# A graph layer's groups taken in a new order, and the last experts' slots cut finer, in one fused kernel

## Chip, cores and metric

One NeuronCore of one Trainium2 chip runs the whole program. The metric is the device time of one execution in microseconds. TensorE (PE) has a granted clock with two levels here, 1.2 and 2.4 GHz, which the profile writes as 0.5 and 1.0.

## The reference

The input is `x`, 128 sequences of 64 tokens with 128 features each (8192 tokens), in float32. Four layers follow, each as `x = x + layer(layernorm(x))`:

1. a spectral graph layer (an eigenbasis of the adjacency, two dense products);
2. a mixture of 8 experts with the top 2 of each token;
3. the second graph layer with an LSTM behind it;
4. a mixture of 8 experts with the top 1 of each token, which share one up projection.

The change touches layers 3 and 4, which are:

```python
# layer 3, first part
h = relu(einsum('ts,bsh->bth', adj, x @ Wg0 + bg0))
h = relu(einsum('ts,bsh->bth', adj, h @ Wg1 + bg1))
for p in 1..4:              # LSTM over windows of p tokens, last state written back
    ...
# layer 4
H = gelu(xf @ W1 + b1)                    # 128 -> 512, one W1 for all experts
probs = softmax(H @ Wg + bg); assign = argmax(probs)
out[token] = probs[token, e] * (H @ Wd[e] + bd[e])   for e = assign[token]
```

## The kernel before

The 8192 tokens are 64 tiles of 128 (`TILES`), and four tiles are a group (`GC` = 512 columns), so there are 16 groups (`GROUPS`). Each layer is a block with a program of its own for each engine; the engines meet at semaphores only, each engine runs its program in the written order, and a block ends before the next begins. `X` (all tokens) stays in SBUF.

**`gnn1` (L1420 to L1605)** is the second graph layer together with the step p = 1 of the LSTM. Its stages for a group g are:

- POOL (L1444) gathers for each token tile two rows of the first experts' result by an indirect DMA (128 gathers in all). There are 8 pairs of buffers (`AHEAD`), so POOL may be two groups ahead.
- DVE `combine` adds both to `X` (L1456, L1458), `stats` takes the tile's statistics (L1463), `scale` (L1469 to L1479, with the inverse root of L1411 to L1417) makes mean and scale of the group.
- ACT `normalized` writes `ZB` (L1529, four instructions). PE makes MIX from it (L1585), ACT copies it to `ZS` (L1553), PE makes UP (L1590, L1591), ACT's ReLU gives HT (L1561), PE makes DN (L1597), DVE `add_bias` gives O (L1487), PE makes MIX2 (L1604), ACT's ReLU gives HS (L1565).
- PE makes the three LSTM gates from HS (GATE, L1576), ACT `gate` applies sigmoid and tanh (L1539), DVE `new_cell` multiplies (L1495), ACT takes the tanh (L1556), DVE `new_state` writes the state into `BIG` (L1500).

The order is written out by hand. PE's turn g is: GATE of group g-1, then MIX, UP, DN and MIX2 of group g. ACT's turn g is: normalized g, gate g-1, ZS g, tanh g-1, HT g, HS g. DVE's turn g is the four tiles of group g; behind the second tile's comes new_cell g-2, behind the third's new_state g-2 and then add_bias g-1; scale g is last.

**`route` (L1101)** gives each token a slot in a list ordered by expert, in which each expert's part is rounded up to whole blocks of `SLOT_TILE` = 256 slots. DVE makes from the counts a table of blocks (`fill`, L1152 and L1154, with `most` = 32 multiples of 256), the slots, and the expert of each block (`te`, L1176 and L1178, with `tiles` x 8 elements on one partition). A loop of one-hot products on DVE, ACT and PE (L1189, L1204, L1218) then lists the tokens by slot, `cols_` columns wide. It is called for layer 2 ("r", 71 tiles of 256) and for layer 4 ("t", 39 tiles of 256, 78 columns).

**`experts` (L1224)** runs over the tiles of 256 slots: POOL gathers the tokens in two halves (L1250, L1254), PE transposes them (L1318), ACT copies (L1292), PE makes the up projection (L1333), ACT's Gelu writes `H` (L1304), PE makes the down projection (L1346) with the weights of the tile's expert, whose number it loads into a register (L1339), DVE adds the expert's bias (L1284, the number loaded at L1279), and SP stores (L1357). On PE the order is: up of tile t, transposes of tile t+1, down of tile t-1. For layer 2 ("c") DVE also copies the expert's up weights for each tile (L1266, L1267); layer 4 ("g") has one up matrix (`w_up_all`). `sweep` writes the first three turns out, puts the middle ones into a hardware loop of two turns, and writes the last ones out.

Of the kernel before, what the change touches and what calls it, by code (L numbers as in the profile page):

```python
# [6 lines left out]
I32 = mybir.dt.int32  # L7
# [4 lines left out]
ds = bass.ds  # L12
# [17 lines left out]
SLOTS0 = (2 * B * N + E * (SLOT_TILE - 1)) // SLOT_TILE * SLOT_TILE  # L30
SLOTS1 = (B * N + E * (SLOT_TILE - 1)) // SLOT_TILE * SLOT_TILE
CONSTS = 11 + E
# [1067 lines left out]

def route(nc, k, sem, tag, choices, slots):  # L1101

# [3 lines left out]
    n = len(choices)  # L1106
    cols_, tiles = slots // P, slots // SLOT_TILE
    most = B * N // SLOT_TILE
    RANK, TOT, LIST, SEATS = k.ps[0], k.ps[1], k.ps[2], k.ps[3]
    s_kept = sem(f"{tag}_kept")  # L1110
    DEEP = 4
    with ExitStack() as own:  # L1112
# [14 lines left out]
        zero = mine("zero", [P, cols_])  # L1127
        block = own.enter_context(nc.Block())

        @block.vector  # L1130
        def _(dve):
# [10 lines left out]
            link(dve.tensor_scalar(steps[:, :], k.irow[:, 0:most], float(SLOT_TILE), None, ALU.mult))  # L1142

# [13 lines left out]
            link(dve.tensor_tensor(off[:, :], end[:, :], nb[:, :], ALU.subtract))  # L1157
            link(dve.scalar_tensor_tensor(out=off[:, :], in0=off[:, :], scalar=float(SLOT_TILE), in1=cnt[:, :],
                                          op0=ALU.mult, op1=ALU.add))
# [36 lines left out]

        @block.scalar
# [9 lines left out]
        @block.tensor  # L1207
        def _(pe):
            pe.wait_ge(marks, 1)
            pe.matmul(RANK[:, :], k.upper[:, :], M[:, :, :].rearrange("p e t -> p (e t)"), start=True, stop=True)  # L1210
            pe.matmul(TOT[:, :], k.ones[:, :], M[:, :, :].rearrange("p e t -> p (e t)"),
                      start=True, stop=True).then_inc(counted, 1)
            pe.matmul(LIST[:, 0:cols_], k.ident[:, :], zero[:, :], start=True, stop=False)
            with pe.Fori(0, TILES * n // DEEP) as i:
                for b in range(DEEP):
                    pe.wait_ge(oh_ready, i * DEEP + (b + 1))
                    pe.wait_ge(ab_ready, i * DEEP + (b + 1))
                    pe.matmul(LIST[:, 0:cols_], above[b][:, :], ohh[b][:, :], start=False, stop=False).then_inc(oh_used, 1)  # L1218
            pe.matmul(LIST[:, 0:cols_], k.ident[:, :], zero[:, :], start=False, stop=True).then_inc(listed, 1)
            pe.wait_ge(s_kept, 1)  # L1220
            pe.matmul(SEATS[:, 0:cols_], k.jump[:, :], summed[:, :], start=True, stop=True).then_inc(listed, 1)


def experts(nc, k, sem, tag, z, y, slots, w_up_all, w_up, w_dn, b_up, b_dn):  # L1224
# [8 lines left out]
    with ExitStack() as own:  # L1233
# [26 lines left out]
        def _(dve):  # L1260
# [9 lines left out]
            def step(t, u, r):  # L1270
# [6 lines left out]
                if not first:  # L1277
                    v, before = 1 - u, r - 1 + u
                    e = dve.value_load(k.expert[0:1, ds(t - 1, 1)], min_val=0, max_val=E - 1)  # L1279
                    dve.wait_ge(dn, t)  # L1280
                    if not (isinstance(before, int) and before < 1):
                        dve.wait_ge(stored[v], before * 16)
                    b2 = b_dn[:, :, :].rearrange("p e d -> p (e d)")[:, ds(e * D, D)]
                    dve.tensor_tensor(ys[v][:, :, :], Y[v][:, 0:HALVES * D].rearrange("p (h d) -> p h d", d=D),  # L1284
                                      b2[:, None, :].to_broadcast([P, HALVES, D]), ALU.add).then_inc(y_ready, 1)
            sweep(dve, step, NT)
# [25 lines left out]
        def _(pe):  # L1312
# [8 lines left out]
            def step(t, u, r):  # L1321
# [16 lines left out]
                if not first:  # L1338
                    e = pe.value_load(k.expert[0:1, ds(t - 1, 1)], min_val=0, max_val=E - 1)  # L1339
                    pe.wait_ge(gelu, t * C)  # L1340
# [3 lines left out]
                    for h in range(HALVES):  # L1344
                        for c in range(C):
                            last = pe.matmul(Y[v][:, h * D:(h + 1) * D], H[v][:, c, h * P:(h + 1) * P],  # L1346
                                             w2[:, ds(e * (C * D) + c * D, D)], start=(c == 0), stop=(c == C - 1))
                    last.then_inc(dn, 1)
# [71 lines left out]
def gnn1(nc, k, sem, y):  # L1420
# [7 lines left out]
    with ExitStack() as own:  # L1428
# [20 lines left out]
        def _(dve):  # L1449
# [52 lines left out]

            for g in range(GROUPS + 2):
                for j in range(GT):
                    if g < GROUPS:
                        combine(g * GT + j)
                        stats(g * GT + j)
                    if j == 1 and g >= 2:
                        new_cell(g - 2)
                    if j == 2:  # L1510
                        if g >= 2:
                            new_state(g - 2)
                        if 1 <= g <= GROUPS:
                            add_bias(g - 1)
                if g < GROUPS:
                    scale(g)
            link.reset()
            dve.wait_ge(hid, GROUPS)

        @block.scalar  # L1520
        def _(act):
# [20 lines left out]

            for g in range(GROUPS + 2):
                u = g % 2
                if g < GROUPS:
                    normalized(g)
                if 1 <= g <= GROUPS:
                    gate(g - 1)
                if g < GROUPS:
# [3 lines left out]
                    act.activation(k.ZS[u][:, :], MIX[u][:, :], ACT.Copy).then_inc(mixed_sb, 1)  # L1553
                if 1 <= g <= GROUPS:
                    act.wait_ge(cell, g)
                    act.activation(tcs[1 - u][:, :], cs[1 - u][:, :], ACT.Tanh).then_inc(tanh_c, 1)  # L1556
                if g < GROUPS:
# [3 lines left out]
                    act.activation(HT[u][:, :], UP[:, :], ACT.Relu).then_inc(h_ready, 1)  # L1561
                    act.wait_ge(mix2, g + 1)
                    if g >= 2:
                        act.wait_ge(fed, g - 1)
                    act.activation(HS[u][:, :], MIX2[:, :], ACT.Relu).then_inc(h2, 1)  # L1565

        @block.tensor
        def _(pe):
            for g in range(GROUPS + 1):
                u = g % 2  # L1570
                if g >= 1:
                    pe.wait_ge(h2, g)
# [4 lines left out]
                    last.then_inc(fed, 1)  # L1577
                if g == GROUPS:
                    break
                pe.wait_ge(z_ready, g + 1)  # L1580
                if g >= 2:
                    pe.wait_ge(mixed_sb, g - 1)
                for j in range(GT):
                    c = slice(j * P, (j + 1) * P)
                    last = pe.matmul(MIX[u][:, c], k.ZB[u][:, c], k.BDAT[:, :], start=True, stop=True)  # L1585
                last.then_inc(mixed, 1)
                pe.wait_ge(mixed_sb, g + 1)
                if g >= 1:
                    pe.wait_ge(h_ready, g)
                pe.matmul(UP[:, :], k.w_g1[:, 0, :], k.ZS[u][:, :], start=True, stop=False)  # L1590
                pe.matmul(UP[:, :], k.b_g1a[:, :], k.adjsum[:, :], start=False, stop=True).then_inc(up, 1)  # L1591
                pe.wait_ge(h_ready, g + 1)
                if g >= 1:
                    pe.wait_ge(o_ready, g)
                for j in range(GT):
                    c = slice(j * P, (j + 1) * P)
                    last = pe.matmul(DN[:, c], HT[u][:, c], k.w_g1[:, 1, :], start=True, stop=True)  # L1597
                last.then_inc(dn, 1)
                pe.wait_ge(o_ready, g + 1)
                if g >= 1:  # L1600
                    pe.wait_ge(h2, g)
                for j in range(GT):
                    c = slice(j * P, (j + 1) * P)
                    last = pe.matmul(MIX2[:, c], O[u][:, c], k.BDAT[:, :], start=True, stop=True)  # L1604
                last.then_inc(mix2, 1)  # L1605

# [157 lines left out]
def gnn_ffn_kernel(nc, x, adj, g0_W1, g0_b1, g0_W2, g0_b2, f0_Wg, f0_bg, f0_W1, f0_b1, f0_W2, f0_b2,  # L1764
# [3 lines left out]
    with ExitStack() as ctx:  # L1768
# [49 lines left out]
        k.sitter = sb("sitter", [P, SLOTS0 // P], I32)  # L1818
        k.expert = sb("expert", [1, SLOTS0 // SLOT_TILE], I32)
        k.st6 = sb("st6", [P, TILES, 6])  # L1820
# [47 lines left out]
        gate0(nc, k, sem, z0)  # L1868
        route(nc, k, sem, "r", [k.K1, k.K2], SLOTS0)
        experts(nc, k, sem, "c", z0, y0, SLOTS0, None, k.w_up0, k.w_dn0, k.b_up0, k.b_dn0)  # L1870
# [3 lines left out]
        gate1(nc, k, sem, z1)  # L1874
        route(nc, k, sem, "t", [k.K1], SLOTS1)
        experts(nc, k, sem, "g", z1, y1, SLOTS1, k.w_up1, None, k.w_dn1, k.b_up1, k.b_dn1)
# [28 lines left out]
```

## Time and profile before

| | us |
|---|---|
| median of three runs | 1786.4 (1785.47 to 1787.1) |
| the profiled execution | 1787.28 |
| its span, first to last instruction | 1785.5 |
| `gnn1`, first gather to last new_state | 793.4 to 1056.5 |
| LSTM steps p = 2 to 4 | 1057 to 1345 |
| `route` for layer 4 | 1493 to 1539 |
| `experts` for layer 4 | 1540 to 1697 |

The profiled execution is 0.9 us above the median, and 1.8 us of it lie outside the span. Over the span PE is busy for 71%, DVE for 47%, ACT for 43% and POOL for 34%, and TensorE's mean granted clock is 0.846. The stages follow each other, so each has to be read by itself: what is saved in one comes off the total as long as nothing moves in the others.

### The profile page before, as it was taken

The numbers are of one execution on the slowest core, as the hardware profiler recorded it, in microseconds if no ns is written. First come the engines' busy times: TensorE is split into PE (matmuls) and PEld (weight loads), VectorE is DVE, ScalarE is ACT, GpSimd is POOL, SyncE is SP. The second block draws the span as 40 slices with busy tenths as digits, with TensorE's granted clock in tenths as the row PEclk, the third lists the DMA queues.
The fourth block names the chain that finished last, engine by engine and source line by source line (L and its number), as shares of the span: only waits on it lengthen the run. The fifth ranks groups of instructions, "written<-read, shape, count | busy, mean of one in ns | idle before, by whom it ended". The sixth has DMA issues, their size and how long they took to land. (4 is left out here: it accounts for less than half of the span.)

```text
span 1785.5 us, 26992 instructions
## 1 busy us (share of the span) xinstructions
PE 1275.3 (71%) x6055; PEld 905.0 (51%) x6056; DVE 836.7 (47%) x3364; ACT 761.6 (43%) x1937; POOL 602.5 (34%) x1091
## 2 busy tenths in 40 slices
PE   2444225577679999966777779989885995799900
PEld 1233225467569999963434433444333453799900
DVE  5777999575842222225565523333336336311122
ACT  3555445111555555433344335444445553555400
POOL 4666145000035566547555200000000000355466
PEclk9999656685789999996688779999997997699955
DMA  9200000002002222221111000000000110122333
GB/s 261 63 1 1 1 1 1 1 24 71 0 25 70 71 71 71 66 56 52 37 37 34 20 1 0 0 0 0 0 0 0 42 47 6 24 69 70 61 94 100
DMA packets 87134, 69.13 MB, mean 39 GB/s; under 512 B 11158, under 2 KB 77020, under 8 KB 87068
## 3 DMA queue, kind: packets, MB, share of 16 engines
q1 hardware_dynamic: 73884, 41.40, 8.1%
q0 software_dynamic: 13184, 27.03, 6.3%
q8 instruction: 20, 0.33, 0.1%
q14 instruction: 46, 0.38, 0.1%
HBM read 41.38 MB, written 27.00 MB: 38 GB/s over the span
## 5 line engine op out<-in xcount | busy, mean ns | idle before, releaser
L1250 POOL COPY g_idx<-sitter 128x1 int32 (+1 forms) x78 | 11.9, 179 | 553.7 <-POOLq L1112 538.1
L1657 PE MATMUL ps<-BIG,w_ihT 128*128 x364 | 162.2, 589 | 20.7 <-ACT e_go L1679 15.0
L1304 ACT ACTIVATE c_H<-ps,c_b 128x256 f32<-128x256 f32 x284 | 117.4, 471 | 131.4 <-PE ps L1333 130.6
L1254 POOL DMA_INDIRECT c_Z<-z,c_idx x142 | 138.6, 976 | 81.0 <-POOLq L1252 57.4
L1444 POOL DMA_INDIRECT d_Y<-y,seat x128 | 129.1, 1009 | 94.5 <-DVE X L1458 49.1
L1346 PE MATMUL ps<-w_dn,c_H 128*128 x1136 | 139.0, 276 | 2.1 <-ACT c_H L1304 2.0
L1333 PE MATMUL ps<-c_ZT,c_w 128*128 128x256 f32 x568 | 136.3, 383 | 1.2 <-ACT c_ZT L1292 1.2
L1346 PEld LDWEIGHTS ps<-w_dn,c_H 128*128 128x128 f32 x1136 | 132.4, 192 | 3.5 <-issue 3.0
L1657 PEld LDWEIGHTS ps<-BIG,w_ihT 128*128 128x128 f32 x364 | 69.3, 194 | 108.6 <-issue 108.6
L1663 PE MATMUL ps<-e_hs,w_hhT 128*128 128x512 f32 (+1 forms) x256 | 110.8, 575 | 12.9 <-DVE e_hs L1709 12.9
L1333 PEld LDWEIGHTS ps<-c_ZT,c_w 128*128 128x128 f32 x568 | 103.6, 192 | 13.4 <-ACT c_ZT L1292 2.0
L1284 DVE TENSOR_TENSOR c_ys<-ps,b_dn 128x256 f32<-128x256 f32 x71 | 30.1, 424 | 155.8 <-PE ps L1346 155.8
L1250 POOL COPY c_idx<-sitter 128x1 int32 (+1 forms) x142 | 21.8, 180 | 238.2 <-POOLq L1112 212.6
L1702 DVE TENSOR_TENSOR e_tmp<-e_gi,e_gg 128x512 f32<-128x512 f32 (+1 forms) x32 | 21.4, 667 | 160.4 <-ACT e_go L1679 160.4
L1304 ACT ACTIVATE g_H<-ps,bias_cols 128x256 f32<-128x256 f32 x156 | 64.6, 471 | 70.8 <-PE ps L1333 70.3
L372 PE MATMUL ps<-h_M,h_xsc 64*128 64x63 f32 (+61 forms) x124 | 37.5, 392 | 76.7 <-POOL h_xsc L217 75.6
L1679 ACT ACTIVATE e_gi<-ps,bias_cols 128x512 f32<-128x512 f32 (+1 forms) x50 | 33.5, 670 | 137.1 <-PE ps L1663 129.2
L1254 POOL DMA_INDIRECT g_Z<-z,g_idx x78 | 74.6, 956 | 43.4 <-POOLq L1252 31.5
L1663 PEld LDWEIGHTS ps<-e_hs,w_hhT 128*128 128x128 f32 x256 | 48.0, 190 | 71.6 <-issue 51.0
L1576 PE MATMUL ps<-d_HS,w_ihT 128*128 128x512 f32 x96 | 75.8, 953 | 11.0 <-ACT d_HS L1565 11.0
L1284 DVE TENSOR_TENSOR g_ys<-ps,b_dn 128x256 f32<-128x256 f32 x39 | 16.6, 424 | 141.5 <-PE ps L1346 141.5
L372 PEld LDWEIGHTS ps<-h_M,h_xsc 64*128 64x128 f32 x124 | 30.8, 308 | 93.3 <-DVE h_M L532 85.6
(495 smaller groups left out, 2951.8 us busy)
## 6 DMA issues: line engine op xcount, KB each, us to landing
y<-c_ys SPq DMA_DIRECT2D x71, 128.0 KB, 1.8
z<-ZB SPq DMA_DIRECT2D x32, 256.0 KB, 2.2
y<-g_ys SPq DMA_DIRECT2D x39, 128.0 KB, 1.8
out_dram<-X SPq DMA_DIRECT2D x32, 128.0 KB, 1.9
c_Z<-z,c_idx POOLq DMA_INDIRECT x142, 2.5
w_up<-in_L_ffn_W_dram SPq DMA_DIRECT2D x1, 2048.0 KB
w_dn<-in_L_ffn_W_dram SPq DMA_DIRECT2D x8, 256.0 KB
w_dn<-in_L_ffn_Wd_dram SPq DMA_DIRECT2D x8, 256.0 KB
```

What stands on the lines that cost most here:

```text
L372: pe.matmul(ps[1][:, r], xsc.to_broadcast([N, P]), M[:, r], start=True, stop=True).then_inc(s_xm, 1)
L1250: pool.tensor_copy(idx[h][u][:, :], k.sitter[:, ds(t * HALVES + h, 1)]).then_inc(copied, 1)
L1254: pool.indirect_dma_start(Z[u][:, h, :], None, z, bass.IndirectOffsetOnAxis(ap=idx[h][u][:, 0:1], axis=0)).then_inc(fetched[u], 16)
L1284: dve.tensor_tensor(ys[v][:, :, :], Y[v][:, 0:HALVES * D].rearrange("p (h d) -> p h d", d=D), b2[:, None, :].to_broadcast([P, HALVES, D]), ...
L1304: act.activation(H[u][:, c, :], UP[u][c // 2][:, c % 2 * SLOT_TILE:(c % 2 + 1) * SLOT_TILE], ACT.Gelu, bias=(b1[u] if w_up is not None els ...
L1333: pe.matmul(UP[u][c // 2][:, c % 2 * SLOT_TILE:(c % 2 + 1) * SLOT_TILE], (w1[u] if w_up is not None else w_up_all)[:, c * P:(c + 1) * P], ...
L1346: last = pe.matmul(Y[v][:, h * D:(h + 1) * D], H[v][:, c, h * P:(h + 1) * P], w2[:, ds(e * (C * D) + c * D, D)], start=(c == 0), stop=(c = ...
L1444: pool.indirect_dma_start(Y[b][f][:, :], None, y, bass.IndirectOffsetOnAxis(ap=k.seat[f][:, n:n + 1], axis=0)).then_inc(fetched[b], 16)
L1576: last = pe.matmul(GATE[n][:, :], k.w_ihT[:, j, :], HS[1 - u][:, :], start=True, stop=True)
L1657: last = pe.matmul(o, k.w_ihT[:, w, :], state(i, u, s, p, wide, lanes), start=True, stop=(s == 0))
L1663: last = pe.matmul(view(k.ps[4 * u + j], wide, lanes), k.w_hhT[:, w, :], view(hs[u], wide, lanes), start=False, stop=True)
L1679: last = act.activation(gates[j][u][:, 0:wide * lanes], k.ps[4 * u + j][:, 0:wide * lanes], ACT.Tanh if j == 2 else ACT.Sigmoid, bias=k.b_ ...
```

## The change

Two edits are put into the kernel together.

The first gives `gnn1` another order. PE's turn g becomes MIX g, MIX2 g-1, UP g, GATE g-1, DN g; ACT's becomes ZS g, HS g-1, HT g, normalized g+1, gate g-1, tanh g-1; DVE's becomes the four tiles with new_state g-3 behind the first, then scale g, add_bias g-1, new_cell g-2. No instruction is added or left out.

The second passes the block size to `route`. For layer 4 it is 128, so each expert's part is rounded up to 128 slots, and the list has 9216 slots (36 tiles of 256) where it had 9984 (39 tiles). The tiles of `experts` stay at 256 slots, but the two halves of one may now belong to two experts: for layer 4 (`kinds` = 2) PE and DVE load two expert numbers for each tile, the down weights are chosen for each half, and the bias is added by two instructions of half the width. Layer 2 is called with the old block size and `kinds` = 1.

```diff
-SLOTS1 = (B * N + E * (SLOT_TILE - 1)) // SLOT_TILE * SLOT_TILE
+SLOTS1 = -(-((B * N + E * (P - 1)) // P * P) // SLOT_TILE) * SLOT_TILE
@@ route
-    cols_, tiles = slots // P, slots // SLOT_TILE
-    most = B * N // SLOT_TILE
+    cols_, tiles = slots // P, slots // block
+    most = B * N // block
@@ experts, vector
-                    e = dve.value_load(k.expert[0:1, ds(t - 1, 1)], min_val=0, max_val=E - 1)
+                    b2 = b_dn[:, :, :].rearrange("p e d -> p (e d)")
+                    kinds = 1 if w_up is not None else HALVES
+                    es = [dve.value_load(k.expert[0:1, ds(t * kinds + (h - kinds), 1)], min_val=0, max_val=E - 1)
+                          for h in range(kinds)]
...
+                    wide = HALVES // kinds
+                    for h in range(kinds):
+                        last = dve.tensor_tensor(ys[v][:, h * wide:(h + 1) * wide, :],
+                                                 Y[v][:, h * wide * D:(h + 1) * wide * D].rearrange("p (h d) -> p h d", d=D),
+                                                 b2[:, None, ds(es[h] * D, D)].to_broadcast([P, wide, D]), ALU.add)
+                    last.then_inc(y_ready, 1)
@@ experts, tensor
-                    e = pe.value_load(k.expert[0:1, ds(t - 1, 1)], min_val=0, max_val=E - 1)
+                    kinds = 1 if w_up is not None else HALVES
+                    es = [pe.value_load(k.expert[0:1, ds(t * kinds + (h - kinds), 1)], min_val=0, max_val=E - 1)
+                          for h in range(kinds)]
...
-                                             w2[:, ds(e * (C * D) + c * D, D)], start=(c == 0), stop=(c == C - 1))
+                                             w2[:, ds(es[h % kinds] * (C * D) + c * D, D)], start=(c == 0), stop=(c == C - 1))
@@ gnn1, vector
-            for g in range(GROUPS + 2):
+            for g in range(GROUPS + 3):
                 for j in range(GT):
                     if g < GROUPS:
                         combine(g * GT + j)
                         stats(g * GT + j)
-                    if j == 1 and g >= 2:
-                        new_cell(g - 2)
-                    if j == 2:
-                        if g >= 2:
-                            new_state(g - 2)
-                        if 1 <= g <= GROUPS:
-                            add_bias(g - 1)
+                    if j == 0 and g >= 3:
+                        new_state(g - 3)
                 if g < GROUPS:
                     scale(g)
+                if 1 <= g <= GROUPS:
+                    add_bias(g - 1)
+                if 2 <= g <= GROUPS + 1:
+                    new_cell(g - 2)
@@ calls
-        route(nc, k, sem, "t", [k.K1], SLOTS1)
+        route(nc, k, sem, "t", [k.K1], SLOTS1, P)
```

ACT's and PE's new turns in `gnn1`, with the semaphore counts each step waits for (the steps themselves are the ones of before):

```
ACT, once ahead of the turns: normalized(0)
ACT, turn g:  ZS(g)            after mixed g+1, up g-1
              HS(g-1)          after mix2 g, fed g-2
              HT(g)            after up g+1, dn g-1
              normalized(g+1)  after scaled g+2, mixed g
              gate(g-1)        after fed g, hid g-2
              tanh(g-1)        after cell g
PE, turn g:   MIX(g)           after z_ready g+1, mixed_sb g-1
              MIX2(g-1)        after o_ready g, h2 g-1
              UP(g)            after mixed_sb g+1, h_ready g
              GATE(g-1)        after h2 g, gated g-1
              DN(g)            after h_ready g+1, o_ready g
```

## Rows read from the trace of the kernel before

**Rows 1.** Busy time by stretch: `gnn1`, layer 4's experts; columns us, busy, PEclk, DMA.

```profile
793.00:1057.00 264.00, 182.24 (x544) 101.22 (x544) 139.19 (x544) 94.02 (x177) 129.12 (x128) 0.73 0.12 32
1549.00:1697.00 148.00, 146.10 (x1009) 135.05 (x1007) 16.18 (x39) 74.97 (x194) 80.82 (x145) 1.00 0.27 67
```

**Rows 2.** Who waited for whom in `gnn1`; columns us in total, times, longest.

```profile
ACT d_HS L1565 <- PE ps L1604: 67.1, 16, 5.0
POOL d_Y L1444 <- DVE X L1458: 49.1, 29, 2.1
```

**Rows 3.** Timeline of one round of `gnn1`; columns start, us, engine, line, what.

```profile
868.23 0.17 DVE L1469 TENSOR_TENSOR ga<-st 128x4 f32<-128x4 f32 x1
...
871.23 0.16 DVE L1479 SCALAR_TENSOR_TENSOR mean<-gm,rstd 128x4 f32<-128x4 f32 x1
871.31 0.34 DVE L1456 SCALAR_TENSOR_TENSOR X<-d_Y,W,X 128x128 f32<-128x128 f32 x1
871.42 1.65 ACT L1529 ACTIVATE ZB<-X,mean,rstd 128x128 f32<-128x128 f32 x4 [1.44 <-DVE mean L1479]
...
872.28 0.35 DVE L1456 SCALAR_TENSOR_TENSOR X<-d_Y,W,X 128x128 f32<-128x128 f32 x1
...
874.74 0.69 ACT L1539 ACTIVATE d_gi<-ps,bias_cols 128x512 f32<-128x512 f32 x1 [1.67 <-PE ps L1576]
...
876.62 0.69 DVE L1495 TENSOR_TENSOR d_cs<-d_gi,d_gg 128x512 f32<-128x512 f32 x1 [3.27 <-ACT d_go L1539]
...
878.20 1.01 DVE L1500 TENSOR_TENSOR BIG<-d_go,d_tc 128x512 f32<-128x512 f32 x1
878.23 1.69 POOL L1444 DMA_INDIRECT d_Y<-y,seat  x1 [1.23 <-DVE X L1458]
...
881.60 0.69 DVE L1487 TENSOR_TENSOR d_O<-ps,b_g1b 128x512 f32<-128x512 f32 x1 [2.39 <-PE ps L1597]
...
885.11 5.49 PE L1576 MATMUL ps<-d_HS,w_ihT 128*128 128x512 f32 x6 [0.69 <-ACT d_HS L1565]
```

**Rows 4.** All of L1479, the end of `scale`: count, duration ns, first and last start.

```profile
L1479 DVE SCALAR_TENSOR_TENSOR mean<-gm,rstd x16: 161/161/164, 809.0 to 1033.1; 128x4 f32<-128x4 f32 x16
```

**Rows 5.** Busy time in a stretch of `gnn1` at full clock (columns as Rows 1).

```profile
911.90:924.90 13.00, 8.49 (x34) 4.55 (x34) 8.79 (x35) 5.68 (x11) 7.57 (x8) 1.00 0.16 42
```

**Rows 6.** Start and end of `gnn1`: gathers, their landing, MIX at half clock, last instruction.

```profile
810.87 2.08 PE L1585 MATMUL ps<-BDAT,ZB 128*128 128x128 f32 x8 [21.01 <-ACT ZB L1529]
...
822.17 0.94 POOL L1444 DMA_INDIRECT d_Y<-y,seat  x1 [0.30 <-issue]
...
DMA to landing us min/median/max: 2.4/2.5/3.4
...
1055.43 1.03 DVE L1500 TENSOR_TENSOR BIG<-d_go,d_tc 128x512 f32<-128x512 f32 x1 [0.69 <-ACT d_tc L1556]
```

**Rows 7.** Timeline of layer 4's experts, PE: two down projections in a row.

```profile
1602.71 1.95 PE L1346 MATMUL ps<-w_dn,g_H 128*128 x16
...
1606.44 1.95 PE L1346 MATMUL ps<-w_dn,g_H 128*128 x16
```

**Rows 8.** PE's sequencer, 1603 to 1606.5: expert number (L1339), addresses (L1346).

```profile
L1339 PEldq ALU_OP  x1: 32/32/32, 1604.4 to 1604.4; - x1
L1339 PEldq TENSOR_LOAD <-expert x1: 301/301/301, 1604.5 to 1604.5; - x1
...
L1346 PEldq FUSED_REGOPS  x4: 46/48/51, 1605.3 to 1605.7; - x4
```

**Rows 9.** Timeline of both routes: block table, expert table (39 and 71 blocks).

```profile
462.02 0.74 DVE L1176 TENSOR_TENSOR r_te<-irow,r_end 1x568 f32<-1x568 f32 x1
...
1500.36 0.42 DVE L1152 TENSOR_TENSOR t_fill<-t_cnt,t_steps 128x256 f32<-128x256 f32 x1
...
1507.56 0.47 DVE L1176 TENSOR_TENSOR t_te<-irow,t_end 1x312 f32<-1x312 f32 x1
```

**Rows 10.** The list loop of layer 4's route, busy time (columns as Rows 1).

```profile
1510.00:1537.30 27.30, 27.30 (x128) 27.30 (x129) 19.95 (x63) 24.75 (x63) 0.00 (x0) 0.50 0.00 0
```

More of the change, by code:

```diff
@@ L1098, in _, with route @@
             sweep(pe, step)
-def route(nc, k, sem, tag, choices, slots):
+def route(nc, k, sem, tag, choices, slots, block):
     marks, counted, oh_ready, ab_ready, oh_used, listed, placed = (
@@ L1127, in route @@
         zero = mine("zero", [P, cols_])
-        block = own.enter_context(nc.Block())
-        @block.vector
+        program = own.enter_context(nc.Block())
+        @program.vector
         def _(dve):
@@ L1141, in _ @@
             link(dve.memset(ones[:, :], 1.0))
-            link(dve.tensor_scalar(steps[:, :], k.irow[:, 0:most], float(SLOT_TILE), None, ALU.mult))
+            link(dve.tensor_scalar(steps[:, :], k.irow[:, 0:most], float(block), None, ALU.mult))
             dve.wait_ge(counted, 1)
@@ L1157, in _ @@
             link(dve.tensor_tensor(off[:, :], end[:, :], nb[:, :], ALU.subtract))
-            link(dve.scalar_tensor_tensor(out=off[:, :], in0=off[:, :], scalar=float(SLOT_TILE), in1=cnt[:, :],
+            link(dve.scalar_tensor_tensor(out=off[:, :], in0=off[:, :], scalar=float(block), in1=cnt[:, :],
                                           op0=ALU.mult, op1=ALU.add))
@@ L1195, in _ @@
             link.reset()
-        @block.scalar
+        @program.scalar
         def _(act):
@@ L1205, in _ @@
                                    bias=before_lo[c][:, ds(t, 1)]).then_inc(ab_ready, 1)
-        @block.tensor
+        @program.tensor
         def _(pe):
@@ L1282, in step @@
                         dve.wait_ge(stored[v], before * 16)
-                    b2 = b_dn[:, :, :].rearrange("p e d -> p (e d)")[:, ds(e * D, D)]
-                    dve.tensor_tensor(ys[v][:, :, :], Y[v][:, 0:HALVES * D].rearrange("p (h d) -> p h d", d=D),
-                                      b2[:, None, :].to_broadcast([P, HALVES, D]), ALU.add).then_inc(y_ready, 1)
+                    wide = HALVES // kinds
[4 more added lines that the diff above has]
+                    last.then_inc(y_ready, 1)
             sweep(dve, step, NT)
@@ L1541, in gate @@
                 last.then_inc(gated, 1)
-            for g in range(GROUPS + 2):
+            normalized(0)
+            for g in range(GROUPS + 1):
                 u = g % 2
[L1545 to L1548, printed above, removed]
                 if g < GROUPS:
@@ L1553, in _ @@
                     act.activation(k.ZS[u][:, :], MIX[u][:, :], ACT.Copy).then_inc(mixed_sb, 1)
-                if 1 <= g <= GROUPS:
-                    act.wait_ge(cell, g)
-                    act.activation(tcs[1 - u][:, :], cs[1 - u][:, :], ACT.Tanh).then_inc(tanh_c, 1)
+                if g >= 1:
+                    act.wait_ge(mix2, g)
+                    if g >= 3:
+                        act.wait_ge(fed, g - 2)
+                    act.activation(HS[1 - u][:, :], MIX2[:, :], ACT.Relu).then_inc(h2, 1)
                 if g < GROUPS:
@@ L1561, in _ @@
                     act.activation(HT[u][:, :], UP[:, :], ACT.Relu).then_inc(h_ready, 1)
[L1562 to L1565, printed above, removed]
+                if g < GROUPS - 1:
+                    normalized(g + 1)
+                if g >= 1:
+                    gate(g - 1)
+                    act.wait_ge(cell, g)
+                    act.activation(tcs[1 - u][:, :], cs[1 - u][:, :], ACT.Tanh).then_inc(tanh_c, 1)
         @block.tensor
@@ L1570, in _ @@
                 u = g % 2
+                if g < GROUPS:
+                    pe.wait_ge(z_ready, g + 1)
+                    if g >= 2:
+                        pe.wait_ge(mixed_sb, g - 1)
+                    for j in range(GT):
+                        c = slice(j * P, (j + 1) * P)
+                        last = pe.matmul(MIX[u][:, c], k.ZB[u][:, c], k.BDAT[:, :], start=True, stop=True)
+                    last.then_inc(mixed, 1)
+                if g >= 1:
+                    pe.wait_ge(o_ready, g)
+                    if g >= 2:
+                        pe.wait_ge(h2, g - 1)
+                    for j in range(GT):
+                        c = slice(j * P, (j + 1) * P)
+                        last = pe.matmul(MIX2[:, c], O[1 - u][:, c], k.BDAT[:, :], start=True, stop=True)
+                    last.then_inc(mix2, 1)
+                if g < GROUPS:
+                    pe.wait_ge(mixed_sb, g + 1)
+                    if g >= 1:
+                        pe.wait_ge(h_ready, g)
+                    pe.matmul(UP[:, :], k.w_g1[:, 0, :], k.ZS[u][:, :], start=True, stop=False)
+                    pe.matmul(UP[:, :], k.b_g1a[:, :], k.adjsum[:, :], start=False, stop=True).then_inc(up, 1)
                 if g >= 1:
@@ L1577, in _ @@
                     last.then_inc(fed, 1)
[L1578 to L1605, printed above, removed]
+                if g < GROUPS:
+                    pe.wait_ge(h_ready, g + 1)
+                    if g >= 1:
+                        pe.wait_ge(o_ready, g)
+                    for j in range(GT):
+                        c = slice(j * P, (j + 1) * P)
+                        last = pe.matmul(DN[:, c], HT[u][:, c], k.w_g1[:, 1, :], start=True, stop=True)
+                    last.then_inc(dn, 1)
 def windows(n_skip):
@@ L1818, in gnn_ffn_kernel @@
         k.sitter = sb("sitter", [P, SLOTS0 // P], I32)
-        k.expert = sb("expert", [1, SLOTS0 // SLOT_TILE], I32)
+        k.expert = sb("expert", [1, max(SLOTS0 // SLOT_TILE, SLOTS1 // P)], I32)
         k.st6 = sb("st6", [P, TILES, 6])
@@ L1868, in gnn_ffn_kernel @@
         gate0(nc, k, sem, z0)
-        route(nc, k, sem, "r", [k.K1, k.K2], SLOTS0)
+        route(nc, k, sem, "r", [k.K1, k.K2], SLOTS0, SLOT_TILE)
         experts(nc, k, sem, "c", z0, y0, SLOTS0, None, k.w_up0, k.w_dn0, k.b_up0, k.b_dn0)
```

## The prediction

> **What bounds the kernel now.** I read the stages first, since they follow each other, and then only the two that the change touches. The second graph layer takes 264 us, in which no engine is full: PE 182, DVE 139, ACT 94, POOL 129 us busy, at a mean granted clock of 0.73, so that the clock is at 1.2 GHz for half the time. Layer 4's experts take 148 us with PE busy for 146 of them at 2.4 GHz [rows 1]. One is bound by a chain between engines, the other by PE.
>
> The waits name the chain: ACT stands 67.1 us in front of HS for MIX2, 16 times, and POOL 49.1 us for buffers that DVE has not read yet [rows 2]; POOL is held back, it is not the bound. The timeline of one round shows why [rows 3]. DVE writes O of the previous group at 881.60, and only behind it come the last tile and `scale` of the present one, whose end lets ACT make ZB. Behind ZB stand, in turn, the gates of the previous group, ZS, UP, HT, DN, and again O. A group's whole way from ZB to O, and the next group's `scale`, thus lie in one loop. From the first end of `scale` to the sixteenth it is 809.0 to 1033.1, 14.94 us a round [rows 4]. In a stretch at 2.4 GHz PE is busy for only 8.49 of 13.0 us [rows 5]; where the clock is at 1.2 GHz the same matmuls take twice as long, and since they lie in the loop, the round grows with them.
>
> **Part 1, the new order.** PE's blocks keep their number and size; what moves is who waits behind whom. In the new DVE turn `scale` g+1 comes ahead of add_bias g, so it needs nothing of PE. I follow one round from the end of `scale` at time 0, all from [rows 3]:
> - ACT makes ZB: 871.39 to 873.07, 1.68.
> - ACT takes the gates of two groups before, whose GATE is long done: from 874.74 to the start of `new_cell` at 876.62, 1.88.
> - new_cell 0.69 (876.62). add_bias, 0.69 (881.60), lies in DVE's wait for the gates.
> - DVE: first tile 0.97 (871.31 to 872.28), new_state 1.01 (878.20), three tiles 2.91. The tanh between new_cell and new_state runs beside the first tile.
> - `scale`: 868.23 to 871.39, 3.16.
>
> The sum is 12.30 us. What is hidden: MIX and MIX2 run beside gates and new_cell; ZS starts at about 5.0 (behind the tanh, which is queued behind the wait for `cell`), UP at 5.7, and UP, GATE and DN need 5.3 us at 2.4 GHz and 10.3 at 1.2 (the blocks as priced in the first rival). DN has until add_bias at 12.3, and even until new_cell at 15.9, before it delays anything, so the clock should fall out of the round. POOL needs 8 gathers of 1.25 us, 10 us a round (0.94 and 0.30 between two; 822.17 being the 24th from 793.4 [rows 6]), so it stays ahead. No wait of the new order is on a DMA that was not waited for before.
>
> The ends: the first end of `scale` stays at 809.0. The third needs the 24th gather, 822.17 + 2.5 to landing [rows 6], a tile and `scale`: 828.8, and nothing of PE. The next round starts up at half clock (MIX 2.08 us [rows 6]); I give it 13.7, between 12.3 and 15. Twelve of 12.3 lead to 990.1. Behind the last end of `scale` come the rest of the chain twice: ZB to UP 5.7, UP, GATE, DN 5.3, O, MIX2, HS 3.1, GATE 2.6, gates, cell, tanh, state 4.4, together 21.1 at 2.4 GHz and some 27 at 1.2; I take 23.5, because the present one has both levels. The stage ends at 1013.6 instead of 1056.5: **-42.9 us**, of which 2.64 x 12 = 32 are the rounds and the rest the first two rounds, which now follow the gathers (19.8 instead of 29.9) while the tail is longer.
>
> **Part 2, fewer tiles.** Two down projections start 3.73 us apart [rows 7], PE without a gap. 39 tiles become 36: **-11.2 us**. Transposes, up and down keep their count in a tile.
>
> **Part 3, what that costs.** In `route`, the block table has 512 elements a lane instead of 256, in two chained instructions, and the expert table 576 instead of 312, in two more. The expert table of 568 takes 0.74 against 0.47 [rows 9], 0.27 for 256 elements; four such instructions, **+1.1 us**, all on the path. The list loop has 72 columns instead of 78. It runs for 27.3 us with the weight loads busy throughout at 1.2 GHz [rows 10]; these do not shrink. It is worth between 0 and 6/78 of 27.3, 2.1 us; I take 0, as the loads carry it.
>
> Each tile loads a second expert number on PE's sequencer. One such sequence lasts from 1604.4 to the first address computation at 1605.3, 0.9 us; the first down matmul runs at 1606.44, so the sequencer is 1.1 us ahead [rows 7, 8]. The second sequence fits into that. Four more address computations of 46 to 51 ns spread over 0.4 us follow, for the second half, while the array works on the first half for 0.9. I take 0; if the cover were gone, it would be 0.9 x 36 = 32 us. DVE's bias add in two halves adds some 0.2 us behind the last tile alone, as DVE is busy for 16 of 148 us [rows 1]; its own second load falls into its wait for PE. Layer 2's experts keep their steps: 0.
>
> **The sum:** -42.9 - 11.2 + 1.1 + 0.2 = -52.8. The profiled execution has 1787.28 us, which gives 1734.5; the median is 0.9 below it, so **1734 us**.
>
> **The rivals.**
>
> *PE becomes the bound of the graph layer.* If the clock stays at 1.2 GHz in the new order, a round cannot be shorter than PE's work: MIX, MIX2 and DN 1.8 each (2.08 less the 0.3 with which one drains), GATE 5.1 (5.49 less it), UP as four of GATE's six, 3.4, together 13.9 [rows 3, 6]. Then 12 rounds and a start of 15 lead to 1010.6, and with 27 to 1037.6: -19, and the total is 1758. For it: the new order lets the array stand for 3 us or so ahead of ZB, and the clock is low half the time now [rows 1]. Against: a stage of such rounds keeps PE busy without a gap at 1.2 GHz, and in this trace such density goes with 2.4 GHz (the experts, [rows 1]). The Trainium skill ("TensorE: Matmul & The Clock Gate", section "Loop structure matters more than you think") says that a loop that keeps the array waiting runs it cold; by it this rival would be the likelier one where my sum has the clock fall out. 12%.
>
> *The second expert number is not hidden.* At full price 32 us: 1766; at the price of the lead being 0.4 us too short, 14 us: 1748. For it: 1.1 against 0.9 is thin, and the loads read SBUF. Against: [rows 7, 8]. 13%.
>
> *Slower: the gathers become the bound.* POOL is released in bursts in the new order, and DVE works more densely beside it. A gather that starts with new_state takes 1.69 instead of 0.94 us (878.23 [rows 3]). If all did, 128 of 2.0 us end at 1049.4, and with landing, a tile, `scale` and the tail (30) the stage ends at 1079, 23 later than now: total 1787.3 + 23 - 9.9 = 1800. It turns to slower where a gather with its gap takes more than 1.9 us on average; now it is 129.1/128 + 0.30 = 1.31 [rows 1]. The Trainium skill ("SBUF — State Buffer", section "Who interferes with whom") has DVE and GpSimd exclude each other on a shared port pair where DVE reads two SBUF operands, and nearly all of DVE's work here does; by it this rival gains. Against: the short DVE instructions beside gathers do not stretch them, and new_state comes once a group as before. 4%.
>
> *No gain,* because something that I don't see holds the round at its length and eats the tiles' gain: 3%, at 1786.
>
> **How the numbers follow.** My forecast has 68%; its own range is 1727 to 1743 (start 12.3 to 15, tail 21 to 27, route 0 to 2.1, and the clock's phase in the later stages, which shift by 50 us). The range of 1726 to 1757 adds the partial cases of the first two rivals and leaves out about 2 in 10. A difference of 0.2%, 3.6 us, is what a measurement of this kernel can tell. Faster: 68 + 12 + 13 = 93%; same 3%; slower 4%.
>
> **What would show it.** The ends of `scale` (L1479 of before) should lie 12.2 to 12.6 us apart, whatever the clock; ACT's wait for MIX2 should nearly vanish; `new_cell` should wait for the gates right behind ZB. The graph layer should end 43 us earlier. Down projections should still start 3.73 us apart, 36 times. I am wrong if rounds take 13.7 or more with PE busy throughout, if "issue" gaps stand ahead of each down projection, or if the gathers last 1.7 us as a rule.

## The result, and the profile after

The changed kernel takes 1740.05 us in the median of four runs (1734.7 to 1742.43), the kernel before 1786.75 in four. The ratio is 0.9729, interval [0.9705, 0.9753]: 46.7 us faster, and inside the forecast range. The profiled execution has 1734.7 us with a span of 1732.9. Span against span that is 52.6 us less, where 52.8 was forecast. It was the quickest of the four; the others were 5.3 to 7.7 us longer and have no profile, so the closeness of the spans flatters the forecast.

By stage, in us, from the first and last instruction of each:

| | before | after | difference | forecast |
|---|---|---|---|---|
| graph layer, first gather to LSTM | 264.0 | 219.0 | -45.0 | -42.9 |
| route for layer 4 | 46.4 | 47.5 | +1.1 | +1.1 |
| layer 4's experts, to the combine's gather | 160.5 | 152.9 | -7.6 | -11.0 |
| everything else | 1314.6 | 1313.5 | -1.1 | 0 |

First the ends of `scale`, the row that answers to [rows 4], then ACT's longest wait and DVE's and POOL's waits in the graph layer (columns as in [rows 2]).

```profile
L1487 DVE SCALAR_TENSOR_TENSOR mean<-gm,rstd x16: 161/161/164, 808.2 to 989.2; 128x4 f32<-128x4 f32 x16
```

```profile
ACT ZB L1536 <- DVE mean L1487: 69.4, 16, 22.0
...
DVE d_cs L1503 <- ACT d_go L1546: 28.5, 15, 4.2
DVE d_O L1495 <- PE ps L1614: 25.0, 11, 5.3
...
POOL d_Y L1452 <- DVE X L1466: 8.5, 6, 1.6
```

The first round starts where it did, and the sixteenth `scale` ends 44 us earlier. ACT no longer stands 67.1 us for MIX2 [rows 2], but 1.1 us once; it now stands for `scale`, and DVE for the gates. That is the loop of the forecast. POOL's wait for DVE has fallen from 49.1 to 8.5 us, since its buffers come free in time. The timeline of one round (columns as in [rows 3]):

```profile
916.02 0.16 DVE L1487 SCALAR_TENSOR_TENSOR mean<-gm,rstd 128x4 f32<-128x4 f32 x1
916.11 0.69 DVE L1495 TENSOR_TENSOR d_O<-ps,b_g1b 128x512 f32<-128x512 f32 x1
916.22 1.65 ACT L1536 ACTIVATE ZB<-X,mean,rstd 128x128 f32<-128x128 f32 x4 [4.01 <-DVE mean L1487]
917.78 0.67 ACT L1546 ACTIVATE d_gi<-ps,bias_cols 128x512 f32<-128x512 f32 x1
...
919.62 0.69 DVE L1503 TENSOR_TENSOR d_cs<-d_gi,d_gg 128x512 f32<-128x512 f32 x1 [2.83 <-ACT d_go L1546]
...
921.21 1.04 DVE L1508 TENSOR_TENSOR BIG<-d_go,d_tc 128x512 f32<-128x512 f32 x1
921.23 1.72 POOL L1452 DMA_INDIRECT d_Y<-y,seat  x1 [1.56 <-DVE X L1466]
...
928.15 0.16 DVE L1487 SCALAR_TENSOR_TENSOR mean<-gm,rstd 128x4 f32<-128x4 f32 x1
```

From 916.02 to 928.15 it is 12.13 us, against 12.30 forecast. All of ACT's and DVE's parts lie in the predicted order: ZB at once, the gates behind it, new_cell behind those, and only one gather a group, the one beside new_state, lasts 1.7 us (in four of the earlier rounds it is two, one of 1.1 beside new_cell and one of 1.5). Two rounds in a row and the whole stage, as busy time (columns as in [rows 1]):

```profile
792.50:1011.40 218.90, 157.11 (x544) 85.65 (x544) 138.82 (x544) 91.40 (x177) 130.19 (x128) 0.80 0.15 39
...
928.20:940.30 12.10, 8.70 (x42) 5.17 (x40) 8.57 (x35) 5.57 (x11) 8.42 (x8) 1.00 0.17 44
940.30:952.40 12.10, 8.70 (x25) 4.30 (x26) 8.50 (x35) 5.57 (x11) 8.42 (x8) 0.79 0.16 43
```

At a granted clock of 1.00 and of 0.79 the round has the same length; a round at 0.62 has it too. Before, the two rounds in which PE was busy for 8.5 us, its work at 2.4 GHz, took 12.9, and the twelve others behind the first 14.7 to 15.5, with PE busy for 11.0 to 12.0. DVE's 139 and POOL's 130 us of work are untouched, and POOL's mean of 1.02 us a gather is that of before [rows 1].

Layer 4's experts, in the middle and at a late tile:

```profile
1514.00:1644.80 130.80, 126.83 (x873) 116.61 (x871) 18.03 (x70) 63.19 (x164) 67.80 (x122) 1.00 0.26 65
```

```profile
1584.73 2.05 PE L1354 MATMUL ps<-w_dn,g_H 128*128 x16 [0.87 <-ACT g_H L1310]
...
1616.25 2.05 PE L1354 MATMUL ps<-w_dn,g_H 128*128 x16 [1.20 <-ACT g_H L1310]
```

PE now stands for 4.0 of 130.8 us where it stood for 1.9 of 148 [rows 1]. Most down projections still start 3.73 us apart [rows 7], but three come 4.77 to 5.10 us behind the one before.

### The profile page after: what moved, and what is told of

Read it like the earlier page. It is cut to its first block and busy times, and to the rows that moved or that the text cites. A ratio compares the mean times of both kernels' runs of the same rounds, so it can differ in the third digit from the quotient of the medians.

```text
span 1732.9 us, 27194 instructions
## 1 busy us (share of the span) xinstructions
PE 1239.7 (72%) x5977; PEld 878.7 (51%) x5978; DVE 839.6 (48%) x3397; ACT 752.5 (43%) x1922; POOL 596.0 (34%) x1079
## 5 line engine op out<-in xcount | busy, mean ns | idle before, releaser
L1339 PE MATMUL ps<-c_ZT,c_w 128*128 128x256 f32 x568 | 136.3, 383 | 1.4 <-ACT c_ZT L1298 1.4
L1339 PEld LDWEIGHTS ps<-c_ZT,c_w 128*128 128x128 f32 x568 | 103.6, 193 | 13.4 <-ACT c_ZT L1298 2.1
L1288 DVE TENSOR_TENSOR c_ys<-ps,b_dn 128x256 f32<-128x256 f32 x71 | 30.2, 425 | 156.0 <-PE ps L1354 156.0
L1689 ACT ACTIVATE e_gi<-ps,bias_cols 128x512 f32<-128x512 f32 (+1 forms) x50 | 33.5, 669 | 137.1 <-PE ps L1673 129.3
L1310 ACT ACTIVATE g_H<-ps,bias_cols 128x256 f32<-128x256 f32 x144 | 59.5, 470 | 70.1 <-PE ps L1339 69.6
L1254 POOL DMA_INDIRECT g_Z<-z,g_idx x72 | 68.7, 954 | 40.0 <-POOLq L1252 29.1
L1288 DVE TENSOR_TENSOR g_ys<-ps,b_dn 128x128 f32<-128x128 f32 x72 | 18.5, 289 | 131.8 <-PE ps L1354 131.6
L1354 PE MATMUL ps<-w_dn,g_H 128*128 x576 | 71.2, 277 | 3.9 <-ACT g_H L1310 3.8
```

Source lines behind the costliest of these rows:

```text
L1254: pool.indirect_dma_start(Z[u][:, h, :], None, z, bass.IndirectOffsetOnAxis(ap=idx[h][u][:, 0:1], axis=0)).then_inc(fetched[u], 16)
L1288: last = dve.tensor_tensor(ys[v][:, h * wide:(h + 1) * wide, :], Y[v][:, h * wide * D:(h + 1) * wide * D].rearrange("p (h d) -> p h d", d= ...
L1310: act.activation(H[u][:, c, :], UP[u][c // 2][:, c % 2 * SLOT_TILE:(c % 2 + 1) * SLOT_TILE], ACT.Gelu, bias=(b1[u] if w_up is not None els ...
L1339: pe.matmul(UP[u][c // 2][:, c % 2 * SLOT_TILE:(c % 2 + 1) * SLOT_TILE], (w1[u] if w_up is not None else w_up_all)[:, c * P:(c + 1) * P], ...
L1689: last = act.activation(gates[j][u][:, 0:wide * lanes], k.ps[4 * u + j][:, 0:wide * lanes], ACT.Tanh if j == 2 else ACT.Sigmoid, bias=k.b_ ...
```

## The experiments

They ran on three chips, on which every kernel takes some 38 us more than in the measurement above (called "at home" here; the record does not name its chip). Most of that lies outside the two edits (last section). So each is compared with the kernel before on its own chip, 1824.77, 1821.34 and 1823.75 us; that kernel has no profile there.

### Each part alone

`again` is the changed kernel. `order_only` is the kernel before with the new `gnn1`; `slots_only` the changed kernel with the old one.

> The changed kernel once more, unchanged. Its profiled execution took 1734.7 us while three unprofiled ones took 1740.0 to 1742.4. If the clock's phase explains the spread, a second profile has the same graph-layer rounds (12.1 us) and the same spacing of down projections, and differs in stages that the change does not touch or in which PE runs at 1.2 GHz for a different time. Rival: the rounds themselves vary. Median 1735 to 1742.

> Only the graph layer's new order; slots and experts as before. My theory: the graph layer gives its 43 to 45 us alone, so 1786.7 - 44 = 1743; rounds of 12.1 us. Rival, that the two edits help each other: less than 40 us.

> Only the finer slots; the graph layer in the old order. My theory: three tiles less at 3.73 us, +1.1 in the route, +3.5 for down projections that start late behind the second expert number: -6.6 us, 1780. Rival, that the late starts belonged to that one profile: -10, 1777.

Measured: `again` 1778.04, ratio 0.9748 [0.9729, 0.9767], 46.7 us less. `order_only` 1784.84, 0.9774 [0.9756, 0.9793], 40 less. `slots_only` 1813.2, 0.9938 [0.9921, 0.9955], 11.6 less. The two add up to 51.5; the 4.8 to the 46.7 are no more than the intervals allow. Both expectations were missed by a little: `order_only` by 3 to 5 us, and `slots_only` gained more than the 6.6 it was given, which lies outside its interval (8 to 14 us). Its rival's 10 us lie inside, but its trace has the late down projections that the rival left out. Its own stages show only some 6 us (153.6 for 160.5 us in layer 4's experts, 1.1 more in the route); where the rest lies is not shown.

The graph layer takes 236.2 us in `again`, 237.3 in `order_only` and 271.5 in `slots_only`: the order gives 34 to 35 us of that stage here. From the third end of `scale` to the sixteenth it is 161.0, 160.1 and 190.2 us, a gain like that at home (192.4 to 161.0). The difference lies in the tail and in the first two rounds. The first takes 29.2 to 30.2 us here in either order (last section), where at home the new order had cut it from 16.3 to 10.0. So within the intervals the two parts are independent, and the order carries most.

### PE's slack in the round

To see whether PE has left the loop, each of GATE's matmuls is made twice, in the new order and in the old:

```diff
-                    for n, j in enumerate(USED):
+                    for n, j in 2 * list(enumerate(USED)):
```

> The changed kernel, each GATE matmul of the graph layer issued twice (the second writes the same values). PE's work in a round grows by 2.6 us at 2.4 GHz or 5.1 at 1.2. If PE stands outside the chain, the rounds stay at 12.1 us as long as the clock is mostly at 2.4, and the time grows by less than 5 us (the tail). Rival, PE in the chain: 2.6 to 5.1 us for each of 15 rounds, 39 to 77 us.

> The same doubling in the kernel before, whose chain holds GATE only as something that MIX queues behind. If PE's blocks lie in its round, the round grows from 14.9 by 2.6 us or more, 40 us in all; if they do not, it stays.

In the old order: 1862.49, ratio 1.022 [1.0195, 1.0245], 41 us above its kernel; rounds of 15.2 to 19.3 us. In the new: 1793.38, 0.9853 [0.9829, 0.9876], some 19 us above the change (0.9853 less 0.9748 of `again`), where under 5 had been expected. In the profiles the stage is 14.8 us longer than in `again` (251.0 for 236.2), and 7.7 of that lie in the tail. Two rounds of the new order:

```profile
922.90:937.80 14.90, 13.92 (x48) 7.25 (x47) 8.65 (x36) 5.69 (x11) 8.43 (x9) 0.94 0.13 36
937.80:949.90 12.10, 10.34 (x36) 5.42 (x35) 8.58 (x34) 5.68 (x11) 8.43 (x8) 0.80 0.15 43
```

Of the thirteen rounds behind the first two, six still took 12.1 us, with 10.3 to 10.5 us of PE; the seven others took 13.0 to 15.1, and each of them lasted 0.98 us longer than PE was busy in it (12.0 to 14.1). So behind the start there are two bounds: the round takes 12.1 us as long as PE has less than about 11.1 us of work in it, and PE's work plus 1.0 beyond that. The changed kernel itself has two such rounds, of 12.6 us with 11.6 of PE. PE is off the chain in the others, with 1 to 2.5 us to spare.

### The chain shortened on DVE

`scale` gets two Newton steps of the inverse root instead of three (its scale is rougher for that), only in the graph layer.

```diff
-    for _ in range(3):
+    for _ in range(2):
```

> The changed kernel with two instead of three Newton steps in the graph layer's inverse root (a slightly rougher scale): three DVE instructions less, 0.59 us, in each scale. If the round is the chain through scale, it falls from 12.1 to 11.5 and the time by 9 us. Rival, gathers or PE: no change.

Measured 1777.12, 0.975 [0.972, 0.9779]: nothing beyond the change, where 9 us had been expected. The rounds:

```profile
882.30:893.80 11.50, 7.77 (x31) 4.11 (x30) 8.09 (x32) 5.28 (x11) 8.40 (x9) 0.77 0.17 45
893.80:908.80 15.00, 13.81 (x48) 7.41 (x48) 8.13 (x33) 6.08 (x12) 8.49 (x9) 0.84 0.15 38
```

```profile
893.61 5.33 PE L1606 MATMUL ps<-d_HS,w_ihT 128*128 128x512 f32 x6
...
899.87 0.69 DVE L1495 TENSOR_TENSOR d_O<-ps,b_g1b 128x512 f32<-128x512 f32 x1 [5.86 <-PE ps L1614]
```

A clean round is 0.6 us shorter, as the chain says. But the next stands at 15.0 with PE busy for 13.8 of it, GATE at half clock (5.33 us) and O waiting 5.86 us for DN; two more take 12.9 with 11.9 of PE, again 1.0 more. From the third end of `scale` to the sixteenth it is 161.0 us as in `again`, and the tail is 3 us longer. Shorten the chain, and the forecast's first rival sets the rounds in which PE works at 1.2 GHz for long.

### Other orders

`late_cell` moves new_cell behind the third tile of the next turn, with tanh ahead of HS; `tanh_behind` puts the tanh behind HT; `best` also moves add_bias behind the first tile of the next turn, and loads layer 2's expert number early.

```diff
@@ late_cell, vector (turns to GROUPS + 4; new_state(g - 4) behind the first tile)
+                    if j == 2 and 3 <= g <= GROUPS + 2:
+                        new_cell(g - 3)
...
-                if 2 <= g <= GROUPS + 1:
-                    new_cell(g - 2)
@@ late_cell, scalar (the same lines go out behind gate)
                 act.activation(k.ZS[u][:, :], MIX[u][:, :], ACT.Copy).then_inc(mixed_sb, 1)
+                if g >= 2:
+                    act.wait_ge(cell, g - 1)
+                    act.activation(tcs[u][:, :], cs[u][:, :], ACT.Tanh).then_inc(tanh_c, 1)
@@ tanh_behind: those three lines stand behind HT instead
@@ best, vector, besides
+                    if j == 0:
+                        if 2 <= g <= GROUPS + 1:
+                            add_bias(g - 2)
```

> The changed kernel with new_cell taken out of the chain between the gates and the next tiles: DVE does it behind the third tile of the next turn, new_state one turn later, ACT's tanh behind the next ZS. If the round of 12.1 us is the chain ZB, gates, new_cell, tiles, scale, it loses DVE's wait for the gates and falls to DVE's own 9.5 us or, as POOL's 8 gathers need 10.0, to about 10.0 to 10.4: 12 rounds of 2 us, 24 us less than the changed kernel. Rival, PE's clock sets the round: it stays at 12 or goes to 13.9 where the clock is at 1.2 GHz.

> Both late_cell and early_numbers: if the parts add up, 2 us less than late_cell.

> late_cell, but with ACT's tanh behind HT instead of ahead of HS. late_cell's trace showed HS and HT queued behind a tanh that waits for the late new_cell, and GATE and DN behind them, so new_cell had come into PE's chain. If that was the fault, rounds go to 10 to 10.5 us where the clock is at 2.4 GHz and to at most 13.9 at 1.2, 10 to 25 us less than the changed kernel. Rival, DVE waits for DN at add_bias because PE is the bound as soon as the round is shorter: rounds near 12 again.

> tanh_behind, add_bias moved behind the first tile of the next turn (1 us more for DN), and the early expert number for layer 2's experts alone, whose stage was 3 to 4 us shorter with it. Graph layer: 1 to 5 us less than tanh_behind if add_bias waits for DN there. Layer 2's experts: 279 instead of 282.5 us.

`late_cell` took 1800.64, 0.9889 [0.987, 0.9908], and with early numbers 1793.11, 0.9843 [0.9819, 0.9867]: both slower than the change, and a miss (24 us less had been expected; the early numbers gave 7.5 us for 2). Its trace:

```profile
908.52 0.63 ACT L1560 ACTIVATE d_tc<-d_cs 128x512 f32<-128x512 f32 x1 [3.71 <-DVE d_cs L1503]
```

The tanh stood 3.7 us for the late new_cell, and HS, GATE and DN, all ready or nearly so, were queued behind it. `tanh_behind` took that wait out, and reached 1788.76, 0.9805 [0.9779, 0.9831], still slower; `best` 1780.79, 0.977 [0.974, 0.98], whose interval reaches that of `again`. Neither beats the change. Two rounds of `best`, and HT and DN in the long one:

```profile
900.50:909.90 9.40, 7.10 (x21) 4.65 (x22) 8.62 (x35) 4.56 (x9) 7.27 (x8) 0.64 0.18 49
909.90:926.10 16.20, 13.10 (x48) 7.79 (x47) 8.78 (x35) 6.69 (x13) 8.76 (x10) 0.89 0.15 39
```

```profile
914.70 0.60 ACT L1571 ACTIVATE d_H<-ps 128x512 f32<-128x512 f32 x1 [5.09 <-remote]
915.35 2.08 PE L1619 MATMUL ps<-w_g,d_H 128*128 128x128 f32 x8 [2.84 <-issue]
```

Without the gates in the loop a round can take 9.4 us, but the next takes 16.2, and two together are 25.6, against 24.2 in the change. PE's 13.1 us at a mixed clock explain only part of the long one: it lasts 3.1 us more than PE is busy, not 1.0. In it HT starts 5.4 us after UP has ended by the profile, and GATE has ended 2.84 us before DN begins. In the changed kernel, and in `again`, HT starts 0.04 us behind UP in each of the sixteen groups. In `best` it does so in eleven; in the five others it starts 4.0 to 7.2 us late, and these are the five rounds of 16.1 to 18.2 us. In `tanh_behind` five groups have it, by 5.3 to 7.6 us. The releaser is named "remote", which stands for no instruction of the profile, and since the ends of matmuls are modelled, UP may have ended later than shown. So what made these two orders slow is not shown, and "PE's work comes due" is only one reading.

### The second expert number

`load_twice_old` is the kernel before, in which PE loads the same number twice for each tile, in both expert layers. `early_numbers` is the changed kernel with PE's loads ahead of its wait for the turned tile.

```diff
@@ load_twice_old
                     e = pe.value_load(k.expert[0:1, ds(t - 1, 1)], min_val=0, max_val=E - 1)
+                    e = pe.value_load(k.expert[0:1, ds(t - 1, 1)], min_val=0, max_val=E - 1)
@@ early_numbers
+                if not first:
+                    es = [pe.value_load(...) for h in range(kinds)]      # arguments as in the change
                 if not end:
                     pe.wait_ge(turned_sb, t + 1)
```

> The kernel before, with PE loading the same expert number twice ahead of each down projection, in both expert layers, and nothing else: 71 + 39 tiles. If the lead of 1.1 us covers a load of 0.7 to 0.9, nothing changes but single late tiles (0 to 0.1 us a tile, under 10 us); if it does not, 0.3 us a tile or more, 33 us. The late starts of 1.0 to 1.4 us that the changed kernel has at four places appear here too if the second load makes them, and not if the finer slots do.

> The changed kernel, with PE's loads of the expert numbers moved ahead of its wait for the transposed tile, where its sequencer stands idle. If the 3.5 us of late down projections come from the two loads between the up and the down projection, they vanish: down projections 3.73 us apart throughout, about 3 us less than the changed kernel. If they come from fetching the longer program, they stay.

`load_twice_old` took 1832.09, 1.0052 [1.0029, 1.0075], 8.3 us more in the medians, over 110 tiles. `early_numbers` took 1775.73, 0.9731 [0.9715, 0.9748]: its interval reaches that of `again`, so the 3 us expected of it are not shown. The clean measure is the time from the first down matmul of a layer to the last; the lines are of before, after, `load_twice_old` and `early_numbers`, in this order (columns as in [rows 4]).

```profile
L1346 PE MATMUL ps<-w_dn,c_H x1136: 272/275/372, 524.9 to 789.6; 128*128 x190
L1346 PE MATMUL ps<-w_dn,g_H x624: 272/275/372, 1553.6 to 1696.5; 128*128 x156
```

```profile
L1354 PE MATMUL ps<-w_dn,g_H x576: 272/275/372, 1508.2 to 1643.9; 128*128 x192
```

```profile
L1347 PE MATMUL ps<-w_dn,c_H x1136: 273/275/372, 525.0 to 795.8; 128*128 x190
L1347 PE MATMUL ps<-w_dn,g_H x624: 273/275/384, 1573.2 to 1717.7; 128*128 x156
```

```profile
L1355 PE MATMUL ps<-w_dn,c_H x1136: 273/275/372, 524.0 to 786.0; 128*128 x190
L1355 PE MATMUL ps<-w_dn,g_H x576: 273/275/276, 1521.3 to 1658.4; 128*128 x192
```

In layer 4 it is 142.9 us before. Three tiles less at 3.73 should leave 131.7; it is 135.7, 134.7 in `again` and 136.2 in `slots_only`. So the change pays 3 to 4.5 us there. The second load alone pays 1.6 (144.5 to 142.9). The three late tiles alone come to 3.8 us at home (1.04, 1.37 and 1.36); the changed kernels have three or four tiles that come more than 4.5 us behind the one before, the kernel before none at home, and `load_twice_old` two (4.77 and 4.89). Why the change has more of them was not tested, nor were its four more address computations apart. In layer 2, where only `load_twice_old` loads twice, it costs 6.1 us (270.8 to 264.7) over 71 tiles, and an early single load gains 2.7 (262.0), in one profile each. For two numbers the early place gains nothing in layer 4 (137.1): the stalls of 1 us go, but 19 of the 35 spacings are 4.03 us or more instead of 3.73.

## Why the prediction was right, and where it was not

**The chain was read right.** The sum of 12.30 us had each member at its place; the round is 12.1, twice 12.6. **The clock falls out** as long as PE's work stays under the chain: 12.10 us at 1.00 and 0.79, and in `again`:

```profile
921.60:933.70 12.10, 8.77 (x42) 5.24 (x41) 8.57 (x35) 5.79 (x11) 8.44 (x8) 1.00 0.17 43
933.70:945.80 12.10, 8.70 (x28) 4.55 (x29) 8.49 (x35) 5.57 (x11) 8.43 (x8) 0.86 0.17 45
```

**The ends.** The third `scale` ended at 828.3, forecast 828.8, with the gathers; the next two rounds took 13.5 and 13.3, where one of 13.7 was forecast; the sixteenth ended at 989.3, forecast 990.1. A second slow round (1.0) and the two of 12.6 made up for nine rounds forecast 0.2 us too long, so that this sum came out closer than its terms. The forecast's 29.9 us for the first two rounds of before are two average ones; they took 31.7. The tail was sized 2 us too long (21.3 against 23.5), which makes most of the difference of -45.0 to -42.9.

**PE as the bound** happened in two rounds, for 0.5 us each, and the margin is small elsewhere. The mean granted clock of the stage was 0.80, so PE still ran at 1.2 GHz for part of it. The Trainium skill ("TensorE: Matmul & The Clock Gate", "Loop structure matters more than you think") says of a loop that keeps the array waiting that it runs cold; the trace agrees on that, with 0.80. What the rule does not decide is whether the cold array is on the path: doubling GATE cost 19 us here and 41 in the old order.

**Fewer tiles** is right in count and price, -11.2, and **route** at +1.1 (46.4 to 47.5, and as much in `slots_only`).

**The step that was mis-sized is "I take 0" for the second expert number.** With what came with it, it measured 3 to 4.5 us in layer 4, about a tenth of the rival's full price of 32. The mistake: 1.1 us of lead was read from a regular tile. With two loads (0.30 us each, two in a row) the lead in such a tile is 0.6:

```profile
L1346 PEldq TENSOR_LOAD <-expert x2: 298/299/300, 1562.7 to 1563.4; - x2
L1354 PEldq FUSED_REGOPS  x8: 46/46/46, 1564.3 to 1565.2; - x8
```

The addresses start at 1564.3, the down matmul at 1564.90. A regular tile is covered by that. A late one is not:

```profile
1610.27 1.70 ACT L1310 ACTIVATE g_H<-ps,bias_cols 128x256 f32<-128x256 f32 x4 [1.82 <-PE ps L1339]
...
L1322 PEldq ALU_OP  x1: 36/36/36, 1614.3 to 1614.3; - x1
L1346 PEldq TENSOR_LOAD <-expert x2: 301/304/308, 1614.5 to 1615.3; - x2
```

The profile puts the wait of the down matmul at 1616.25 down to `g_H`, but the H it reads was done at 1611.97. What came late was a gather: L1322 waits ahead of the transposes for the tokens of the next tile, the last of them landed at 1614.23, 4.1 us after its gather began instead of the usual 2.6, and PE's sequencer passed L1322 0.03 us later. Its lead is gone then, so both loads and the first address follow in series, 2.0 us to the down matmul. All three late tiles have this: landings at 1582.63, 1614.23 and 1630.62, each passed 0.03 us later. The kernel before has one such late tile. There the one load takes 1.2 us of the same way (landing at 1680.77, down matmul at 1681.99), and it lost 0.35 (4.08 against 3.73) where the changed kernel lost 1.04 to 1.37; in `order_only`, with one load too, such a tile lost 0.86.

**The gathers** never came near the bound. The Trainium skill ("SBUF — State Buffer", "Who interferes with whom") has a DVE instruction with two SBUF inputs contend with a GpSimd instruction that reads SBUF. The trace agrees: a gather that starts while new_state runs lasts 1.5 to 1.7 us instead of 0.94, and one that starts in new_cell 1.1. It is lengthened by less than what is left of the DVE instruction then (0.2 us for 0.3 left), so the short ones of `combine` (0.35 us) cost next to nothing, and the mean stays 1.02.

**The total.** -45.0 + 1.1 - 7.6 - 1.1 is -52.6 in the profiled run, and the medians differ by 46.7. Where the other runs of the changed kernel spent their 5 to 8 us is open. The steps p = 2 to 4 of the LSTM, which the change does not touch, took 298.8 us in both profiles at home (1057.4 to 1356.2 before; the 1345 of the table ahead is too early) but 302.2 in `again`, 299.7 in `slots_only` and 305.4 in `late_cell`. That may be the forecast's "clock's phase in the later stages", and it is large enough, but the unprofiled runs do not show whether it was that. That the profiled run was the quick one, and so hit the forecast span to 0.2 us, is luck; the medians missed by 6 (1740 for 1734), inside the range.

## What to carry to other kernels

In a hand-written order, follow one round as a loop and ask of each engine's program what a ready step is queued behind. Moving the wait for the longest branch a turn later takes that branch out of the loop, until another engine's own work is the loop. Before shortening a chain further, double the work of the engine that looks free: the rounds that keep their length show how much slack it has. A lead of a sequencer is to be read in the tiles whose input lands late, not in the regular ones, and a releaser that the profile names is to be checked against the time at which it was done.

## What was not expected of the hardware

All kernels took some 38 us more on the chips of the experiments. The stages put it in two places. The last stage, the combine behind layer 4's experts, took 107.8 us instead of 85.1; the first round of the graph layer 29.5 instead of 10.0 (30.2 instead of 16.3 in the old order). In both stages of `again`, small DVE instructions stand apart, here in the first round's `scale`, where 0.2 us was usual:

```profile
830.72 0.16 DVE L1424 TENSOR_TENSOR d_root<-d_root,rstd 128x4 f32<-128x4 f32 x1 [1.23 <-DVE d_root L1423]
832.12 0.16 DVE L1425 SCALAR_TENSOR_TENSOR rstd<-d_root,rstd 128x4 f32<-128x4 f32 x1 [1.24 <-DVE d_root L1424]
```

Each lasts 0.16 us as always; they start 1.4 us apart. The second round is not longer for it, 7.7 us. The first round was long in all twelve kernels there (19.7 to 30.4 us), but not always in this way: in `slots_only` it is one wait of 21.1 us, `add_bias` for DN, ended by "remote". The cause was not found. It may be the chips or the time at which they ran, and ratios between chips are compared with that in mind.
